# A gated cross-attention and feed-forward block: attention outputs turned by DMA instead of TensorE, and a subtraction moved from VectorE to GpSimd

## The reference

```python
# _L0_xattn_ref, _L0_ffn_ref and the last lines of reference(), shortened
q, k, v = heads(layernorm(x) @ Wq), heads(ctx @ Wk), heads(ctx @ Wv)        # 16 heads of 32
attn = softmax(where(mask, q @ k.T * 32 ** -0.5, -max))
x = x + tanh(g_xattn) * (attn @ v) @ Wo
xq = fake_quant(layernorm(x))                    # one scale for the whole tensor, 8 bits
h = fake_quant(silu(xq @ fq(w_gate).T) * (xq @ fq(w_up).T))
x = x + tanh(g_ffn) * (h @ fq(w_down).T)
```

## Time and profile before

| | us |
|---|---|
| median of 3 executions | 624.25 (623.23 to 624.53) |
| the profiled execution | 623.66 |
| its span, first to last instruction | 621.8 |
| TensorE busy in the span | 600.3 (97%) |
| VectorE busy | 518.7 (83%) |
| ScalarE busy | 375.9 (60%) |
| GpSimd busy | 230.3 (37%) |

### The profile page before, as it was taken

How to read it: one execution, slowest core, us unless ns; L and a number is a source line. 1 busy time by engine, 2 the same in 40 slices (tenths; PEclk the granted TensorE clock), 3 DMA queues, 4 the chain that set the end, 5 groups by cost and what they waited for, 6 DMA issues and landing times. The chain is left out here.

```text
span 621.8 us, 12091 instructions
## 1 busy us (share of the span) xinstructions
PE 600.3 (97%) x3706; PEld 447.8 (72%) x3727; DVE 518.7 (83%) x958; ACT 375.9 (60%) x484; POOL 230.3 (37%) x472
## 2 busy tenths in 40 slices
PE   8999999999999999999999986999999999899997
PEld 6798999999999999999999873444444444444544
DVE  6778889999999998999899757888888888866765
ACT  5464677777777777778675435555555553455653
POOL 7112454454544444535433103111011110067775
PEclk9999999999999999999999998999999999899999
DMA  8538834454444344535642000396643110199633
GB/s 312 171 114 245 178 82 103 82 98 98 90 88 97 92 90 101 113 76 109 130 102 59 16 0 10 72 251 226 205 153 92 35 34 1 46 365 400 238 118 119
DMA packets 118459, 77.89 MB, mean 125 GB/s; under 512 B 98163, under 2 KB 100621, under 8 KB 118413
## 3 DMA queue, kind: packets, MB, share of 16 engines
q1 hardware_dynamic: 113169, 60.51, 37.9%
q10 hardware_dynamic: 5244, 16.82, 7.9%
HBM read 32.48 MB, written 21.36 MB: 87 GB/s over the span
## 5 line engine op out<-in xcount | busy, mean ns | idle before, releaser
L1447 ACT ACTIVATE sb_silu<-ps_g,sb_sgu 128x512 f32<-128x512 f32 x88 | 60.5, 687 | 72.4 <-PE ps_g L1542 43.0
L1542 PE MATMUL ps_g<-sb_xqT,sb_wgu 128*128 128x512 bf16 x344 | 89.3, 379 | 1.0 <-DVE sb_xqT L1498 0.6
L1542 PE MATMUL ps_u<-sb_xqT,sb_wgu 128*128 128x512 bf16 x346 | 89.4, 379 | 0.3
L1513 DVE SCALAR_TENSOR_TENSOR sb_h<-ps_u,sb_sgu,sb_silu 128x512 f32<-128x512 f32 (+1 forms) x88 | 66.1, 751 | 19.8 <-PE ps_u L1542 18.9
L1064 PE MATMUL ps_q<-sb_xT_hi,sb_wq_hi 128*128 128x256 f32 x256 | 75.4, 295 | 0.7 <-DVE sb_q_lo L765 0.6
L629 ACT ACTIVATE sb_prob<-sb_prob 128x616 f32<-128x616 f32 x64 | 45.6, 713 | 47.9 <-DVE sb_prob L791 47.9
L1623 POOL TENSOR_TENSOR sb_wgu<-sb_wgu,sb_x 128x512 f32<-128x512 f32 x31 | 53.4, 1722 | 54.1 <-DVE sb_wgu L1680 54.0
L1066 PE MATMUL ps_q<-sb_xT_hi,sb_wq_lo 128*128 128x256 f32 x256 | 72.4, 283 | 0.0
L1065 PE MATMUL ps_q<-sb_xT_lo,sb_wq_hi 128*128 128x256 f32 x256 | 72.3, 283 | 0.0
L1747 PE MATMUL ps_z<-sb_wdT,sb_hq 128*128 128x512 bf16 x324 | 71.4, 380 | 0.3
L1517 DVE TENSOR_REDUCE sb_hmax<-sb_h 128x1 f32<-128x512 f32 (+1 forms) x88 | 60.4, 686 | 7.6
(11 more groups left out here) (238 smaller groups left out, 1421.4 us busy)
## 6 DMA issues: line engine op xcount, KB each, us to landing
h_spill<-sb_h SPq DMA_DIRECT2D x4, 2816.0 KB, 9.2
sb_h<-h_spill ACTq DMA_DIRECT2D x16, 704.0 KB, 6.7
out_dram<-sb_wgu SPq DMA_DIRECT2D x31, 256.0 KB, 2.4
sb_x<-in_x_dram ACTq DMA_DIRECT2D x1, 4096.0 KB, 18.8
sb_w_in<-in_L_ffn_w_gate_dram SPq DMA_DIRECT2D x11, 256.0 KB, 2.7
sb_w_in<-in_L_ffn_w_up_dram SPq DMA_DIRECT2D x11, 256.0 KB, 2.5
sb_x<-in_x_dram SPq DMA_DIRECT2D x2, 1024.0 KB, 14.6
sb_x<-in_x_dram SPq DMA_DIRECT2D x2, 512.0 KB, 4.5
```

The source lines that it names most:

```text
L1447: act.activation(silu[(j * KI + i) % 2][:, :, :].rearrange("p t n -> p (t n)"), p_g[(j * KI + i) % 2][:, :], ACT.Silu, scale=sgu[:, i:i + ...
L1513: dve.scalar_tensor_tensor(steps_h, p_u[(j * KI + i) % 2][:, :, :], sgu[:, KI + i:KI + i + 1], silu[(j * KI + i) % 2][:, :, :], ALU.mult, ...
L1542: last = pe.matmul(banks[(j * KI + i) % 2][:, :], wgu[:, what, k, i * P:(i + 1) * P], xqT[j][:, k, :], start=(k == 0), stop=(k == KD - 1))
```

## The change

Four things change in the attention.

1. Outputs of tiles 4 to 27 are no longer transposed by TensorE. GpSimd splits `o_sb` into planes in buffer `ppl_u` (`out_split`), SyncE's DMA turns them back into `o_sb` (`outs_transposed`), ScalarE joins the planes and then casts the high part (`out_high`), and VectorE subtracts from the joined tile in SBUF instead of from PSUM (`out_part`). `ppl_u` is now shared by probabilities and outputs, so waits are added: the split of the probabilities waits for the DMA of the outputs, the DMA of the probabilities waits for VectorE's `out_part`, and the split of the outputs waits for the DMA of the probabilities.
2. The low parts of tiles 8 to 31 are subtracted by GpSimd (`x_low`), at the end of its slot, instead of by VectorE at the end of its own.
3. In ScalarE's slots 4 to 29 the join of the probabilities comes first, and the cast of the outputs comes after the first exponential. VectorE's `out_part` moves from ahead of the row maxima to ahead of the second `scores_sub`.
4. TensorE's `project(n-2)` is no longer split around `outputs(n-1)`; all of it comes last.

Semaphores `v_xlo`, `t_oT` and `t_ck` are renamed or merged (`x_lo_in`, `o_turned`, `t_c`).

```diff
+OUT0, OUT1 = 4, NT - 4
...
+                o_u = o_sb[:, :].bitcast(U16)
+                o_pairs = o_u.rearrange("p (n two) -> p two n", two=2)
+                o_planes = o_u.rearrange("p (two n) -> p two n", two=2)
+                opl_planes = ppl_u[:, 0, 0:2 * D].rearrange("p (two n) -> p two n", two=2)
+                oT_pairs = ppl_u[:, 1, 0:2 * D].rearrange("p (n two) -> p two n", two=2)
+                oT_whole = ppl_u[:, 1, 0:2 * D].bitcast(F32).rearrange("p (k n) -> p k n", k=KD)
...
+                def out_by_dma(m):
+                    return not isinstance(m, int) or OUT0 <= m < OUT1
...
                         sp.wait_ge(g_ppl, n - PROB0 + 1)
                         sp.wait_ge(a_p, 2 * n)
+                        if out_by_dma(n - 2):
+                            sp.wait_ge(v_olo, n - 1)
                         sp.dma_start_transpose(ppl_u[:, 1, :].rearrange("p (c n) -> p c n", n=P),
                                                ppl_u[:, 0, :]).then_inc(d_pT, 16)
+
+                    def outs_transposed(m):
+                        if out_by_dma(m):
+                            sp.wait_ge(g_opl, m - OUT0 + 1)
+                            sp.dma_start_transpose(o_u.rearrange("p (c n) -> p c n", n=P),
+                                                   ppl_u[:, 0, 0:2 * D]).then_inc(d_oT, 16)
...
                         rows(w)
+                        outs_transposed(w - 2)
...
                         wait(pool, a_exp, 2 * n + 1)
                         wait(pool, d_pT, 16 * (n - PROB0))
+                        if out_by_dma(n - 2):
+                            wait(pool, d_oT, 16 * (n - 1 - OUT0))
                         pool.tensor_tensor(carry[:, :], eps[:, :], minus[:, :], ALU.mult)
                         pool.tensor_copy(ppl_planes[:, :, 0:HW], prob_pairs).then_inc(g_ppl, 1)
+
+                    def out_split(m):
+                        wait(pool, v_o, 2 * m + 2)
+                        wait(pool, d_pT, 16 * (m + 2 - PROB0))
+                        pool.tensor_tensor(carry[:, :], eps[:, :], minus[:, :], ALU.mult)
+                        pool.tensor_copy(opl_planes, o_pairs).then_inc(g_opl, 1)
+
+                    def x_low(n, t):
+                        wait(pool, a_xhi, n + 1)
+                        wait(pool, x_lo_in, n)
+                        wait(pool, t_q, n - t % 2 - 2)
+                        cols = slice(t % 2 * P, (t % 2 + 1) * P)
+                        pool.tensor_tensor(xT_lo[t // 2][:, :, cols], xpl_T, xT_hi[t // 2][:, :, cols].bitcast(F32),
+                                           ALU.subtract).then_inc(x_lo_in, 1)
...
                                 pool.tensor_copy(w_bf[:, 0:size], wd_i8[q][:, 0:size]).then_inc(g_wdb, 1)
+                        if runs(n - 1, NT) and out_by_dma(n - 1):
+                            out_split(n - 1)
+                        if runs(n + 4, NT) and joined(n + 4):
+                            x_low(n + 4, t)
...
+                    def out_high(m):
+                        wait(act, t_y, m)
+                        if out_by_dma(m):
+                            wait(act, d_oT, 16 * (m + 1 - OUT0))
+                            wait(act, a_p, 2 * m + 4)
+                            act.copy(oT_pairs, o_planes).then_inc(o_turned, 1)
+                            wait(act, o_turned, m + 1)
+                            act.copy(oT(m)[0], oT_whole).then_inc(a_ohi, 1)
+                        else:
+                            wait(act, o_turned, m + 1)
+                            act.copy(oT(m)[0], p_x[:, :, :]).then_inc(a_ohi, 1)
...
+                    def behind_planes(n, t):
+                        prob_join(n - 1)
+                        prob_copy(n - 1, 1)
+                        row_abs(n - 4)
+                        exponential(n, 0)
+                        out_high(n - 2)
+                        if runs(n + 2, NT):
+                            q_part(n + 2, (t + 2) % 4)
+                        exponential(n, 1)
+                        ahead(n, t)
...
-                        dve.tensor_tensor(o_lo, p_x[:, :, :], o_hi.bitcast(F32), ALU.subtract).then_inc(v_olo, 1)
+                        whole = oT_whole if out_by_dma(m) else p_x[:, :, :]
+                        dve.tensor_tensor(o_lo, whole, o_hi.bitcast(F32), ALU.subtract).then_inc(v_olo, 1)
...
-                        if runs(n - 2, NT - 1):
+                        outputs_late = by_dma(n - 1) and not last_by_dma(n)
+                        if runs(n - 2, NT - 1) and not outputs_late:
                             out_part(n - 2)
...
                             dve.reciprocal(w_inv[:, :], w_am[:, :]).then_inc(v_winv, 1)
+                        if outputs_late:
+                            out_part(n - 2)
...
-                        if runs(n + 4, NT):
+                        if runs(n + 4, NT) and not joined(n + 4):
                             x_part(n + 4, t)
...
-                        out_transpose(n - 2)
+                        if not out_by_dma(n - 2):
+                            out_transpose(n - 2)
                         prob_transpose(n - 1, 1)
...
                         scores(n, t, 1)
-                        project(n - 2, [0])
                         outputs(n - 1, 0)
                         outputs(n - 1, 1)
-                        project(n - 2, range(1, KD))
+                        project(n - 2)
```

More of the change, by code:

```diff
@@ L514, in deviation @@
                             wait(pool, a_xn, n)
-                            wait(pool, v_xlo, n - 1)
+                            wait(pool, x_lo_in, n - 1)
                         else:
@@ L550, in slot @@
                             wait(pool, a_xn, n + 5)
-                            wait(pool, v_xlo, n + 4)
+                            wait(pool, x_lo_in, n + 4)
                             x_split()
@@ L639, in prob_join, with row_abs, ahead @@
                         act.copy(pT_pairs, ppl_T).then_inc(a_p, 1)
+                    def out_high(m):
[9 more added lines that the diff above has]
+                            act.copy(oT(m)[0], p_x[:, :, :]).then_inc(a_ohi, 1)
+                    def row_abs(m):
+                        wait(act, g_nb2, m + 1)
+                        wait(act, v_xmax, m + 1)
+                        if isinstance(m, int) and m + 4 >= PLANES_FREE:
+                            act.wait_ge(x_lo_in, NT)
+                        else:
+                            wait(act, v_x1, m + 2)
+                        act.activation(xabs(m), row(m), ACT.Abs, bias=nb2[:, span(m)],
+                                       scale=rs2[:, span(m)]).then_inc(a_abs, 1)
+                    def ahead(n, t):
+                        if runs(n + 4, NT):
+                            if joined(n + 4):
+                                x_join(n + 4, t)
+                            else:
+                                x_part(n + 4, t)
+                        if runs(n + 5, NT):
+                            normalise(n + 5, t + 5)
+                    def behind_planes(n, t):
[8 more added lines that the diff above has]
+                        ahead(n, t)
                     def slot(n, t):
+                        if runs(n - 1, NT) and by_dma(n - 1) and not last_by_dma(n):
+                            behind_planes(n, t)
+                            return
                         if last_by_dma(n):
@@ L649, in slot @@
                         if runs(n - 2, NT):
-                            wait(act, t_oT, n - 1)
+                            wait(act, o_turned, n - 1)
                             if not late_tile(n - 2):
@@ L656, in slot @@
                         if runs(n - 1, NT) and not (isinstance(n, int) and n == 2):
-                            if not by_dma(n - 1) and not (isinstance(n, int) and n == NT - 1):
+                            if not last_by_dma(n) and not (isinstance(n, int) and n == NT - 1):
                                 prob_copy(n - 1, 0)
@@ L660, in slot @@
                         if runs(n - 4, NT - 1):
[L661 to L668, removed]
+                            row_abs(n - 4)
                         if runs(n, NT):
                             exponential(n, 0)
-                        if runs(n - 1, NT) and by_dma(n - 1) and not last_by_dma(n):
-                            prob_join(n - 1)
                         if runs(n + 2, NT):
@@ L1069, in x_transpose @@
                         wait(pe, a_xn, n + 1)
-                        wait(pe, v_xlo, n)
+                        wait(pe, x_lo_in, n)
                         for k in range(KD):
@@ L1077, in queries @@
                         if part == 0:
-                            wait(pe, v_xlo, m - t % 2 + 2)
+                            wait(pe, x_lo_in, m - t % 2 + 2)
                             wait(pe, v_qlo, m)
@@ L1277, in _ @@
                                              start=True, stop=True)
-                    last.then_inc(t_ck, 1)
+                    last.then_inc(t_c, 1)
```

29 lines of the change are left out of this document (16 added, 13 removed).

## The result

The changed kernel takes 653.29 us (median of 4, 652.72 to 655.40) against 624.35 before: 1.0474 times as long, 95% interval 1.0458 to 1.0490. That is slower, as forecast, 9 us more than the 644 predicted and inside the range. The profiled execution took 655.4 us with a span of 653.6. Lines of after.py in the rows: queries and project L1144, `x_low` L572, `out_split` L564 and L565, the join and cast of the outputs L691 and L693, `out_part` L892, `outputs_norm` L881, DMA of the outputs L449.

The account below looks back on a forecast made before the run. TensorE sets the 10.58 us slot; with the late low part a pair takes 22.64 against 21.16: 1.48 x 12 = 17.8, first pair -0.4, w_down +3.1, sum +20.5, so 644 us, range 627 to 656.

Parts of the forecast that it names:

- Transposes removed, a slot of 10.14: TensorE in slots 6 to 29: transposes of 0.44 us go, leaving 10.14 of 10.58 us if nothing else is in the way.
- By load every engine fits; order decides: Attention slot: ScalarE 9.3, VectorE 9.3 and GpSimd 7.6 us all fit in 10.14, so only order decides.
- The late low part: `x_low` behind `out_split` on GpSimd comes late, stopping TensorE's queries in 12 even slots, some 1.9 to 2.4 us each.
- The round trip alone, 10.72 a slot: Rival: the outputs' loop through GpSimd, DMA, ScalarE and VectorE sets slots, +0.14 x 24 = +3.4, 627.6 us; chance 0.06.
- The forecast's pair: An even and an odd attention slot together, from queries to queries: 22.64 us against 21.16 before, 1.48 longer.
- Stops cost no clock: TensorE in the attention: stops leave the granted clock at the 2.4 GHz level, as with 7.82 of 10 us busy.
- w_down, +3.1 in slots 22 on: Last three pairs: VectorE quantises w_down between maximum and normalisation, 4.0 us in all, some 0.9 already paid, +3.1.
- Regrouping `project` at nothing: TensorE's projection in the attention: regrouping changes only the order of the same matmuls, costed at nothing.
- A blocked port at `out_part`: Rival: VectorE's `out_part` meets GpSimd's split of the probabilities, up to 1.21 us a pair, typically +7, 652; chance 0.09.

Follow-up runs that it names:

- experiment 6: The changed kernel with the low parts back on VectorE and the output norms ahead of VectorE's `q_part` and statistics: 649.26 us, 1.0413.
- experiment 1: The changed kernel with the low parts of the tokens' rows back on VectorE, last in its slot; outputs still by DMA: 657.7 us, 1.0549.
- experiment 7: The changed kernel with one DMA queue line moved, the first w_down rows issued ahead of the outputs of tile 20: 653.82 us, 1.0493.
- experiment 9: experiment 6 plus experiment 7's order, DMA for even tiles 4 to 26 only: 629.40 us; tiles 4 to 18, old tail order: 623.51, `project` split there too: 620.94.
- experiment 8: The changed kernel's new orders alone, no output turned by DMA and the low parts on VectorE: 625.70 us, 1.0035.
- experiment 3: The changed kernel with GpSimd's last two steps exchanged, low part ahead of the split of the outputs: 668.14 us, 1.0703.
- experiment 4: The kernel of experiment 1 with a second 1.04 us copy and another small operation in `out_split`: 686.33 us, 1.1009.

## Why the prediction was right in sign and place, and where a step failed

*Transposes removed, a slot of 10.14.* Right: 10.14 in the last windows, where nothing else holds TensorE.

*By load every engine fits; order decides.* Right for the changed kernel. In experiment 6 load may decide after all: VectorE is full there, with 0.49 us a slot through a blocked port.

*The late low part.* Twelve stops in the slots foretold; the subtraction takes 1.29 us on average (1.26 taken), the split 1.04. As what happens this was right, as the main cause of the loss it failed: experiment 1 takes all twelve stops away and gains nothing, because the round trip behind them takes 22.36 of the 23.12 us of a pair by itself, and the edit lengthens it by 0.38 us a slot. Of their 1.7 us each the stops cost 0.75.

*The round trip alone, 10.72 a slot (rival, 627.6).* This is the term that was mis-sized. Measured it is 11.03 and 11.33. For the second: `out_part` to last norm 4.52 (4.34 taken, with a wait of 0.22 in it), GpSimd 1.32 (1.34), from there to the join 3.47 (DMA of 3.0 taken, and 0.04 to wake), join to the next `out_part` 2.02 (2.00 without the wake). The DMA's way is 0.43 of the 0.6: its price came from the earlier trace rows, a transpose of the same size, 3.0 from issue to landing; the outputs' take 3.3 in the steady slots (x14 in the view of DMA issues below), the issue comes 0.03 behind the split, and the join some 0.1 later behind the landing than the 0.04 taken. With 11.2, so 0.6 above 10.58, the rival would have read 624 + 24 x 0.6 = 638, and its chance would have been much more than 0.06. The forecast's pair held one round trip and one stop. Up to the split's end its chain was right (10.62 us behind the queries, 10.65 measured), the join came 0.46 late, and that is nearly all of what lies between its 22.64 and the 23.12 measured.

*Stops cost no clock.* Wrong. The earlier trace rows showed a window with 7.82 of 10 us busy at full clock, and the even slots are busier than that, yet in three of them the clock fell to the lower level or near it right behind a stop of 1.7 to 2.9 us (the granted clock is also 0.50, so 1.2 GHz, from 278.94 to 280.94 and from 330.08 to 332.08). In slot 18 that costs about 1.5 us. In slots 22 and 26 TensorE loses as much, but other work is as late there: VectorE waits until 281.76 for the first w_down rows, and in slot 26 the cast of the outputs ends only 0.06 us ahead of `out_part`. What the clock costs in these two is open.

*w_down, +3.1 in slots 22 on.* Too small: with the pairs' share 9 were predicted there, 16.0 measured. The trace shows the round trip there as well: from tile 21 on every `out_part` starts 0.03 to 0.06 us behind the end of ScalarE's cast, so it waits for nothing else. The queue was left out: the outputs' DMAs share it with `down_rows`. In tiles 22, 24 and 26 the way from the split's end to the join takes 5.21, 5.44 and 4.99 us, against some 3.4 in the tiles up to 19. Tile 22, and from the view of DMA issues the landing of its DMA and of those from 92 to 245 us:

```profile
300.21 1.04 POOL L565 COPY sb_ppl<-sb_o_sb 128x1024 uint16<-128x1024 uint16 x1
300.50 0.43 SPq L495 DMA_DIRECT2D sb_w_in<-in_L_ffn_w_down_dram  x1
...
301.95 1.54 SPq L449 DMA_TRANSPOSE sb_o_sb<-sb_ppl  x1
...
306.46 1.35 ACT L691 COPY sb_ppl<-sb_o_sb 128x1024 uint16<-128x1024 uint16 x1 [3.33 <-issue]
```

```profile
sb_o_sb<-sb_ppl SPq DMA_TRANSPOSE x1, 4.4
sb_o_sb<-sb_ppl SPq DMA_TRANSPOSE x14, 3.3
```

The DMA is issued 0.70 us behind the split's end, after the rows, and lands 4.4 us later instead of 3.3. In three tiles that makes an estimated 5.4 of the missing 7 us. It is read from the trace and not shown by a run: moving the first rows gave nothing (experiment 7), and experiment 9 shows only that outputs by DMA and the w_down stretch don't go together.

*Regrouping `project` at nothing.* True with the new order of ScalarE (experiment 8, steady slots); with the old one it costs 0.2 us a slot (623.51 against 620.94).

*A blocked port at `out_part`.* Not seen there: 0.68 us on average, 0.67 before. It appears where VectorE keeps the low part, 0.38 us in experiment 1 and 0.49 in 6. So the move of the low part to GpSimd was worth something after all, against a VectorE that does it beside the split.

## What to carry to other kernels

A wait that stands 12 times in the profile need not be the loss: follow what the waiting work feeds, and ask how long the loop would be with the wait gone. Here a second loop was only 0.75 us shorter per pair, and removing the visible stop uncovered it. A transfer that turns one tile's result and comes back within the slot closes a loop through every engine; give it two slots (every second tile). Here, away from the slots with w_down, that was worth 3.2 of the 3.5 us that the removed work took.

## What the runs showed of the hardware that was not expected

TensorE's granted clock fell from 2.4 GHz to near 1.2 right behind stops of only 1.7 to 2.9 us, with TensorE busy for 10.4 us of each slot before; the other nine stops of 1.2 to 2.3 us left it at full clock. Over the span it was 0.984 here, 0.979 in experiment 1, 0.966 in experiment 3 and 0.955 in experiment 4, with 27.0, 28.9, 32.0 and 42.9 us of stops at the queries and `project`. VectorE's subtraction of two SBUF inputs and a GpSimd operation that reads SBUF held each other up by 0.38 us (experiment 1) and 0.49 us (experiment 6) on average, the one that began later waiting.
